# A conditioned expert FFN on one core: two more sets of weights through seven block products

## What is computed

```python
# stage 1, "conditioning": FFN 256 -> 1024 -> 256 with relu, weights corrected by LoRA
# (common and expert factors of rank 16 each; the expert is given per sequence)
Wi = wi + 2 * (common_wi_b @ common_wi_a + experts_wi_b[id] @ experts_wi_a[id])
Wo = wo + 2 * (common_wo_b @ common_wo_a + experts_wo_b[id] @ experts_wo_a[id])
y = relu(x @ Wi.T) @ Wo.T
# stage 2: router on the mean over the tokens, softmax, the two best of 8 experts, shares w
p = softmax(mean(y, tokens) @ gate_w);  (e1, w1), (e2, w2) = top2(p), shares normed to 1
out = x + sum_k w_k * (gelu(y @ w1[e_k] + b1[e_k]) @ w2[e_k] + b2[e_k])
```

## Time and profile before

| what | value |
|---|---|
| median of 3 runs | 270.0 us (268.86 to 270.25) |
| the profiled execution, its time / its span | 269.23 us / 267.4 us |
| busy: PE, PEld | 98%, 80% |
| busy: DVE, ACT, POOL | 61%, 64%, 55% |
| TensorE clock granted, mean | 0.999 |
| DMA, mean rate over the span | 73 to 74 GB/s, 17.43 MB read and 2.10 MB written |

### The profile page before, as it was taken

The page is one execution under the profiler, slowest core; times in us unless marked ns, Lnnn a source line. Parts: engine busy times, 40 slices in busy tenths (PEclk is TensorE's granted clock), DMA queues, the critical chain, the costliest instruction groups (busy, mean ns, idle before and its releaser), DMA issues.

```text
span 267.4 us, 3575 instructions
## 1 busy us (share of the span) xinstructions
PE 262.0 (98%) x1156; PEld 213.4 (80%) x1156; DVE 162.3 (61%) x269; ACT 171.0 (64%) x275; POOL 146.2 (55%) x178
## 2 busy tenths in 40 slices
PE   6999999999999999999999999999999999999994
PEld 2778888888888888888888788888788888888883
DVE  0883624323498826667595787557866567665664
ACT  2757334455526469988986887676677676774650
POOL 2176244373836877798539999466356366331100
PEclk9999999999999999999999999999999999999999
DMA  5995120210032012202202112203202105000004
GB/s 175 357 388 194 42 78 0 82 39 2 0 122 78 6 73 79 81 1 78 81 0 58 37 67 78 78 0 79 70 12 80 66 15 196 0 0 4 0 0 157
DMA packets 11138, 19.75 MB, mean 74 GB/s; under 512 B 2000, under 2 KB 2256, under 8 KB 10992
## 3 DMA queue, kind: packets, MB, share of 16 engines
q1 hardware_dynamic: 10544, 18.61, 21.0%
q10 hardware_dynamic: 576, 0.92, 1.0%
HBM read 17.43 MB, written 2.10 MB: 73 GB/s over the span
## 4 chain that ended last, share of the span: by engine, by line
PE 96%; DMA 1%; SPq 1%; DVE 0%; issue 0%; DVEq 0%
PE out_ps L693 16%; PE out_ps L694 16%; PE out_ps L697 16%; PE hid_ps L693 14%; PE hid_ps L694 14%; PE hid_ps L697 14%; DMA lora_first<-in_early 1%; PE hid_ps L736 1%; PE out_ps L814 1%; PE hid_ps L740 1%; PE hid_ps L744 1%; PE hid_ps L826 1%; PE hid_ps L836 1%; SPq L296 1%; DVE x_sb L1133 0%
## 5 line engine op out<-in xcount | busy, mean ns | idle before, releaser
L398 POOL TENSOR_TENSOR up_lo<-up_raw,up_hi 128x512 fp32r<-128x512 f32 x39 | 50.6, 1316 | 51.4 <-ACT up_hi L529 51.4
L693 PE MATMUL out_ps<-hid_hi,down_hi 128*128 128x512 f32 x192 | 74.9, 390 | 0.0
L694 PE MATMUL out_ps<-hid_lo,down_hi 128*128 128x512 f32 x192 | 74.8, 389 | 0.0
L697 PE MATMUL out_ps<-hid_hi,down_lo 128*128 128x512 f32 x192 | 74.8, 389 | 0.0
L693 PE MATMUL hid_ps<-act_hi,up_hi 128*128 128x512 f32 x168 | 65.8, 391 | 0.0
L694 PE MATMUL hid_ps<-act_lo,up_hi 128*128 128x512 f32 x168 | 65.6, 390 | 0.0
L697 PE MATMUL hid_ps<-act_hi,up_lo 128*128 128x512 f32 x168 | 65.4, 389 | 0.0
L561 ACT ACTIVATE hid_ps<-hid_ps,bias_sb 128x512 f32<-128x512 f32 x64 | 42.2, 659 | 29.6 <-DVE hid_ps L981 19.1
L957 DVE SCALAR_TENSOR_TENSOR hid_lo<-hid_ps,mix,hid_hi 128x512 fp32r<-128x512 f32 x64 | 47.8, 747 | 18.7 <-ACT hid_hi L575 18.2
L404 POOL TENSOR_TENSOR down_lo<-down_raw,down_hi 128x512 fp32r<-128x512 f32 x24 | 31.6, 1317 | 41.4 <-ACT down_hi L539 41.3
L575 ACT ACTIVATE hid_hi<-hid_ps,mix 128x512 fp32r<-128x512 f32 x64 | 44.1, 689 | 4.6
(11 more groups left out here) (89 smaller groups left out, 214.0 us busy)
## 6 DMA issues: line engine op xcount, KB each, us to landing
up_raw<-in_w SPq DMA_DIRECT2D x16, 256.0 KB, 2.8
down_raw<-in_w SPq DMA_DIRECT2D x16, 256.0 KB, 2.6
lora_raw<-in_lora SPq DMA_DIRECT2D x10, 256.0 KB, 5.3
down_raw<-in_woT SPq DMA_DIRECT2D x8, 256.0 KB, 3.5
up_raw<-in_wiT SPq DMA_DIRECT2D x7, 256.0 KB, 4.6
outT<-x_sb SPq DMA_DIRECT2D x6, 256.0 KB, 3.6
x_sb<-in_xT SPq DMA_DIRECT2D x1, 1024.0 KB, 8.9
x_sb<-in_xT SPq DMA_DIRECT2D x1, 512.0 KB, 5.8
```

What stands on the lines that cost most here:

```text
L398: ins = eng.tensor_tensor(up_lo[:, n, cols], up_raw[:, n, cols], f32(up_hi[:, n, cols]), ALU.subtract)
L693: eng.matmul(out, w_h, a_h, start=start, stop=False, skip_group_check=onto)
L694: eng.matmul(out, w_h, a_l, start=False, stop=False, skip_group_check=onto)
L697: return eng.matmul(out, w_l, a_h, start=False, stop=stop, skip_group_check=onto)
```

## The change

Sets 4 and 5 become seven sets too. For that:

- the token sums of sequence 1 are made on POOL in sets 1 and 2, their high parts on ACT in set 2, their low parts on DVE in set 3; all four `raw_low` of sequence 1 stand in set 2;
- `weight_sums(4)` and `weight_sums(5)` stand on POOL in sets 2 and 3, behind the merge of their LoRA product, and the up product of set 4 is made in set 2 (a second up factor there) and that of set 5 in set 3;
- in a seven set of the conditioning the factor products and the logits stand at other places in PE's order (down factor after down pair 2), and use bank 0 instead of 3;
- the router's reduction out of bank 0 gets a semaphore of its own (`s_read`), and the rest of that step (`router_max`) comes later;
- ACT's and DVE's order in sets 4 and 5 is written anew, and POOL's in sets 1 to 4.

```diff
-    PLAIN = range(N_COND)
+    PLAIN = [n for n in range(N_COND) if n not in (SETS, SETS + 1)]
     PLAIN_TILES = [(0, 0), (1, 0), (0, 1), (1, 1)]
...
+    UP_FACTOR_AT = {0: [1], 1: [2], 2: [3, 4], 3: [5], 5: [6], 6: [7]}
     PRODUCTS = []
     for n in range(N_COND):
-        if n + 1 < N_COND:
-            PRODUCTS.append(("u", n + 1))
-        PRODUCTS.append(("d", n))
+        ups = [("u", to) for to in UP_FACTOR_AT.get(n, ())]
+        PRODUCTS += ups[:1] + [("d", n)] + ups[1:]
...
+    def products_to(q):
+        return max(product_count("d", q), *(product_count("u", to) for to in UP_FACTOR_AT.get(q, [1])))
...
     RAW_HI_AT = {1: [(0, 0), (0, 1)], 5: [(1, 0), (1, 1)], 9: [(2, 0)], 10: [(2, 1)]}
-    RAW_LO_AT = {2: [(0, 0), (0, 1)], 3: [(0, 2), (0, 3)], 6: [(1, 0), (1, 1), (1, 2), (1, 3)],
+    RAW_LO_AT = {2: [(0, 0), (0, 1), (0, 2), (0, 3)], 6: [(1, 0), (1, 1), (1, 2), (1, 3)],
                  11: [(2, 0), (2, 1)], 12: [(2, 2), (2, 3)]}
-    SUM_AT = {5: [(1, 0), (1, 1), (1, 2), (1, 3)], 9: [(2, 0), (2, 1)], 10: [(2, 2), (2, 3)]}
-    SUM_HI_AT = {6: [(1, 0), (1, 1)], 12: [(2, 0)], 13: [(2, 1)]}
-    SUM_LO_AT = {7: [(1, 0), (1, 1), (1, 2), (1, 3)], 13: [(2, 0), (2, 1)], 14: [(2, 2), (2, 3)]}
-    LORA_HI_AT = {1: [(0, 4)], 2: [(1, 0), (1, 1)], 3: [(1, 2), (1, 3)], 4: [(1, 4)]}
-    LORA_LO_AT = {0: [(0, 2)], 1: [(0, 4)], 2: [(1, 0)], 3: [(1, 1), (1, 2)], 4: [(1, 3), (1, 4)]}
+    SUM_AT = {1: [(0, 0), (0, 1)], 2: [(0, 2), (0, 3)], 5: [(1, 0), (1, 1), (1, 2), (1, 3)], 9: [(2, 0), (2, 1)], 10: [(2, 2), (2, 3)]}
+    SUM_HI_AT = {2: [(0, 0), (0, 1)], 6: [(1, 0), (1, 1)], 12: [(2, 0)], 13: [(2, 1)]}
+    SUM_LO_AT = {3: [(0, 0), (0, 1), (0, 2), (0, 3)], 7: [(1, 0), (1, 1), (1, 2), (1, 3)], 13: [(2, 0), (2, 1)], 14: [(2, 2), (2, 3)]}
+    LORA_HI_AT = {1: [(0, 4), (1, 0)], 2: [(1, 2), (1, 1)], 3: [(1, 3)], 4: [(1, 4)]}
...
+        s_read = sem("s_read")
...
             b = READY_SEQ[p]
-            eng.wait_ge(s_sum_hi, 2 * (p - 1) + m // 2 + 1)
+            eng.wait_ge(s_sum_hi, 2 * p + m // 2 + 1)
             eng.tensor_tensor(act_lo[:, b, 4 + m, :], t_sum[:, m, :], f32(act_hi[:, b, 4 + m, :]),
...
                 w, n = up_raw[:, q % NU, :], q % NU
-                eng.wait_ge(s_up_raw[n], 16 * (q // NU + 1))
+                if cond(q):
+                    eng.wait_ge(s_merge, product_count("u", q))
+                else:
+                    eng.wait_ge(s_up_raw[n], 16 * (q // NU + 1))
                 eng.tensor_tensor(w[:, block(S3)], w[:, block(0)], w[:, block(1)], ALU.subtract)
...
                 if m == 0:
-                    eng.wait_ge(s_y, NT * KD * p)
-                    if p > 1:
-                        eng.wait_ge(s_sum_lo, 4 * (p - 1))
+                    if p == 0:
+                        eng.wait_ge(s_x1, 16)
+                    else:
+                        eng.wait_ge(s_y, NT * KD * p)
+                        eng.wait_ge(s_sum_lo, 4 * p)
                 if m in (2, 3):
-                    eng.wait_ge(s_t, 4 * (p - 1) + (1 if m == 2 else 3))
+                    eng.wait_ge(s_t, 4 * p + (1 if m == 2 else 3))
                 left = [(0, 1), (1, 1), (1, 1), (1, 0)][m]
...
-            def lora_lows(q):
-                for b, lot in LORA_LO_AT.get(q, ()):
-                    lora_low(b, lot)
...
             after((s_down_lo, 1))
-            lora_lows(0)
+            lora_low(0, 2)
             for q in range(1, NSET):
-                if q < N_COND - 1:
+                if q == 1:
+                    up_low(2)
+                    down_low(1)
+                    after((s_down_lo, 2))
+                    lora_low(0, 4)
+                    token_sums(1)
+                    after((s_t, 2))
+                    lora_low(1, 0)
+                elif q == 2:
+                    up_low(3)
+                    token_sums(2)
+                    down_low(2)
+                    after((s_down_lo, 3))
+                    lora_low(1, 2)
+                    weight_sums(4)
+                elif q == 3:
+                    up_low(4)
+                    weight_sums(5)
+                    down_low(3)
+                    after((s_down_lo, 4))
+                    lora_low(1, 1)
+                    lora_low(1, 3)
+                elif q == 4:
+                    up_low(5)
+                    down_low(4)
+                    after((s_down_lo, 5))
+                    lora_low(1, 4)
+                elif q < N_COND - 1:
                     if q in TOTAL_AT:
...
                     token_sums(q)
-                    if q in LORA_LO_AT:
-                        after((s_down_lo, q + 1))
-                        lora_lows(q)
                 elif q == N_COND - 1:
...
                 if b and t == 0:
-                    eng.wait_ge(s_t, 4)
+                    eng.wait_ge(s_t, 8)
                     eng.wait_ge(s_raw_lo, 8)
...
                 b = READY_SEQ[p]
-                eng.wait_ge(s_t, 4 * (p - 1) + 2 * (n + 1))
+                eng.wait_ge(s_t, 4 * p + 2 * (n + 1))
                 eng.activation(act_hi[:, b, 4 + 2 * n:6 + 2 * n, :], t_sum[:, 2 * n:2 * n + 2, :], ACT.Copy)\
...
                         up_high(q + 1)
+                    if q == SETS:
+                        up_high(q + 1)
                 if q - 2 in GROUP_LAST[0:NB]:
...
                         term_high(LOGITS_AT[q])
-                    up_high(q + 1)
-                    hid_high(q, 1)
-                    down_high(q)
                     if q - 1 in GROUP_LAST[0:NB]:
                         cond_out(GROUP_LAST.index(q - 1), 0)
-                    hid_high(q, 2)
+                    if seven(q):
+                        hid_high(q, 1)
+                        if q > SETS:
+                            up_high(q + 1)
+                        hid_high(q, 2)
+                        down_high(q)
+                    else:
+                        up_high(q + 1)
+                        hid_high(q, 1)
+                        down_high(q)
+                        hid_high(q, 2)
                     if q + 1 == N_COND:
...
                 if bank == 0 and q - 1 in LOGITS_AT:
-                    eng.wait_ge(s_nmax, LOGITS_AT[q - 1] + 1)
-                if bank == 3 and 1 <= q < N_COND:
-                    eng.wait_ge(s_merge, product_count("d", q))
+                    eng.wait_ge(s_read, LOGITS_AT[q - 1] + 1)
+                if bank == 0 and 0 < q <= N_COND and seven(q - 1):
+                    eng.wait_ge(s_merge, products_to(q - 1))
+                if bank == 3 and 1 <= q < N_COND and not seven(q):
+                    eng.wait_ge(s_merge, products_to(q))
...
                 eng.wait_ge(s_up_hi, q)
-                if q == SETS:
-                    eng.wait_ge(s_raw_lo, 4)
-                if q == N_COND:
-                    eng.wait_ge(s_raw_lo, 8)
-                    eng.wait_ge(s_sum_lo, 4)
-                if q == N_COND + TOP_K * SETS:
-                    eng.wait_ge(s_raw_lo, 12)
-                    eng.wait_ge(s_sum_lo, 8)
+                if q in GROUP_FIRST[1:]:
+                    eng.wait_ge(s_raw_lo, 4 * GROUP_FIRST.index(q))
+                    eng.wait_ge(s_sum_lo, 4 * GROUP_FIRST.index(q))
...
+            def factors_to(q):
+                bank = 0 if seven(q) else 3
+                return hid_ps[:, bank, :], (s_hid_lo, 4 * q + 1 if seven(q) else 4 * q)
             def next_up_factor(q):
-                if q + 1 < N_COND:
-                    eng.wait_ge(s_hid_lo, 4 * q)
-                    up_factor(q + 1, hid_ps[:, 3, 0:SW], hid_ps[:, 3, SW:2 * SW])
+                bank, free = factors_to(q)
+                for to in UP_FACTOR_AT.get(q, ())[:1]:
+                    eng.wait_ge(*free)
+                    if q in LOGITS_AT and seven(q):
+                        eng.wait_ge(s_read, LOGITS_AT[q] + 1)
+                    up_factor(to, bank[:, 0:SW], bank[:, SW:2 * SW])
...
                 if q < N_COND:
-                    if q + 1 < N_COND:
-                        eng.wait_ge(s_merge, product_count("u", q + 1))
+                    bank, free = factors_to(q)
+                    if q in UP_FACTOR_AT:
+                        eng.wait_ge(s_merge, product_count("u", UP_FACTOR_AT[q][0]))
                     else:
-                        eng.wait_ge(s_hid_lo, 4 * q)
-                    down_factor(q, hid_ps[:, 3, :])
+                        eng.wait_ge(*free)
+                    down_factor(q, bank)
+            def later_up_factor(q):
+                bank, _ = factors_to(q)
+                for to in UP_FACTOR_AT.get(q, ())[1:]:
+                    eng.wait_ge(s_merge, product_count("d", q))
+                    up_factor(to, bank[:, 0:SW], bank[:, SW:2 * SW])
...
                     down(q - 1, 1)
+                    if cond(q):
+                        router_logits(q)
                     one_of_seven(q, "m5", 3, True)
+                    if cond(q):
+                        next_up_factor(q)
```

(42 more changed lines are left out.)

## The result

The changed kernel took 272.43 us in the median (270.37 to 275.02, 16 runs), the kernel before in the same session 270.25 (268.86 to 273.33, 16 runs). The ratio is 1.0061, with a 95% interval of 1.0031 to 1.0090: slower, by 0.8 to 2.4 us. Three runs of the changed kernel and one of the kernel before lie over 1.5% above the fastest of their kernel and don't count in the ratio; without them the medians are 272.10 and 270.25. Forecast were 272.1 us and "slower by over 0.5%" as the likeliest case.

What follows compares the result with a forecast made beforehand. PE, busy 98% of the span, was taken as the bound. New waits less the removed matmuls gave +1.64 us, POOL in set 4 +0.5: +2.1 on the median 270.0, so 272.1 us, range 269.6 to 273.4.

Steps and rivals of the forecast that it cites:

- Removed: Sets 4 and 5 on PE: two up products fewer, 6 matmuls, 1.36 us saved.
- Logits: Set 5: PE waits 0.25 us ahead of the router logits for hid_low(5,0), which stands behind third_sum(5) on DVE.
- Up factor 7, by raw_high on ACT: Set 6: hid_high(5,3), queued behind two raw_high, comes later; PE waits 0.77 us.
- The chain beside the token sums: Set 6: the router's tiny DVE operations wait for POOL's token sums, putting merge_up(7) at 78.12.
- The open price: Router's two-input DVE operation in set 6: net +0.2 if it passes POOL, +1.64 us if it waits; the wait was taken.
- Down factor 6: Set 6: PE waits 1.90 us for merge_up(7), which follows the router's stretched chain on DVE.
- Last up tile: Set 6: PE waits 0.36 us for merge_down(6), which follows merge_up(7) by 3.33 us on DVE.
- POOL in sets 1 to 4: POOL's added work and collisions with eight DVE lows make PE wait 0.5 us at down pair 0 of set 4.
- Rival 1: Few collisions: router's chain not stretched, POOL in time in set 4; 269.8 to 270.7 us, chance 0.27.
- Rival 2: Set 6: hid_high(5,3) on ACT isn't late and PE never waits; 268.6 us, chance 0.08.
- Rival 3: POOL bounds already in sets 3 and 4, collisions at their upper end; 272.9 to 273.8 us, chance 0.15.
- set 6 lasted its old 11.4 us: Sign on PE's timeline: set 6 keeping its earlier length of 11.4 us would show the prediction wrong.

Runs made afterwards that it cites:

- set4_only: Changed kernel with set 5 plain again, so only set 4 takes seven products; ratio to the kernel before 0.9984, stretch on PE 0.68 us shorter.
- pool_raw_swap: Changed kernel with token sums sooner on POOL, raw_high later on ACT, and hid_low(5,0) ahead of third_sum(5) on DVE; median 268.64 us, ratio to the kernel before 0.9947.
- pool_early: Changed kernel with POOL's token sums of set 5 sooner, three ahead of up_low(6), the fourth ahead of down_low(5); ratio to the kernel before 0.9962.
- before_tok_late: Kernel before with POOL's four token sums of set 5 held until hid_low(5,3) is done; ratio to the kernel before 1.0099.
- raw_late: Changed kernel with ACT's two raw_high of set 5 moved behind hid_high(6,0); ratio to the kernel before 1.0057.
- before_b: Kernel before, unchanged, in a second profiled execution; stretch on PE 60.13 us against 60.15 in the first.

## Why the prediction was right, and where not

The time (272.1 against 272.43) and the sign were right, and so was the way there, but for one term: 0.5 us of wait for POOL in set 4, which did not come. That the time came within 0.3 us is in part luck: without that term the sum gives 271.6, and the ratio puts the changed kernel at 271.9.

- **Removed:** 6 matmuls, 1.36 us. Right: `set4_only` shows half of it, `pool_raw_swap` all.
- **Logits:** a wait of 0.25; measured 0.30.
- **Up factor 7, by raw_high on ACT:** 0.77; measured 0.70 with its aftermath. hid_high(5,3) was forecast 2.11 us behind the start of set 6 and came 1.97 behind (71.48 to 73.45).
- **The chain beside the token sums:** forecast 4.86 us from hid_low(5,3) to merge_up(7), measured 4.77. The open price, whether the two-input operation (L1081) waits for POOL, was settled: 1.00 us, ended with a token sum; 0.23 in `pool_early`. By the Trainium skill's page SBUF — State Buffer (Who interferes with whom) it had to wait, and the trace agrees.
- **Down factor 6:** 1.90; measured 1.79. **Last up tile:** 0.36; measured 0.39. The four waits sum to 3.28 forecast, 3.18 measured.
- **POOL in sets 1 to 4, the term that was mis-sized:** I took 0.5 us of wait at down pair 0 of set 4, "nearer to the upper end". Measured: nothing. down_low(3) ended at 49.87, where PE needed it near 51.5; 1.6 us were in hand. The eight lows on DVE cost POOL far less than the 0.65 each that I took: from lora_low at 25.31 to the end of down_low(3) are 24.56 us, 2.9 more than my count of POOL's work (21.7), so by estimate 0.36 for each of the eight. The timelines show that the two engines shared the price: the low that DVE began at 28.71 took 1.30 us, to 30.01, past the end of POOL's second token sum (29.46), and POOL's lora_low, begun at 29.54, took 1.87 instead of 1.53. In all the eight lows took DVE about 1.9 us more than their own time. `set4_only` confirms that nothing is lost there.
- So the sets came to +1.83 where the forecast had 1.64 + 0.5 (the waits less the matmuls and less 0.1 of an old wait give 1.72; 0.1 I can't place). The ratio's 1.65 us (0.8 to 2.4) holds both.

Rival 1 (few collisions) asked for a chain that isn't stretched; here it was stretched, from 3.60 to 4.77 us. Rival 2 needed ACT 0.8 us sooner. Rival 3 needed a late POOL; it was on time. The prediction was to be wrong if set 6 lasted its old 11.4 us; it lasted 14.35.

What stays open: the rest of the timed difference of `pool_early` (-0.4 us at a full clock, where its stretch says 0.0; the scatter of these runs allows as much), and whether the wait of 1.7 us in the changed kernel ever brings the clock down. In its two profiles it did not, and 11 of its 16 timed runs had a mean clock of 0.998 or more, which leaves no room for a fall of 3.4 us; the other five can have theirs from the start-up.

## What to carry to other kernels

When an edit moves one instruction of the bounding engine later (here a factor product, by 3 us), follow what each other engine has queued behind that instruction's consumer, for a whole stage on. Two engines that wait for one another's instructions, as DVE and POOL do here, need their timelines laid beside one another: a chain of tiny operations that takes 3.0 us alone (`pool_early`) took up to 6.3 beside the other engine's long ones. And cure a wait together with what lies behind it: moving `raw_high` alone brought 0.65 us, both cures with the swap brought 3.3 (all in the stretch).

## What the runs showed of the hardware

- DVE operations with two SBUF inputs (L1081, 227 ns alone) and eight-column TENSOR_SCALARs waited for POOL's current instruction of 1.25 us, and took up to 1.29 us each (`before_tok_late`). What did not wait, in the changed kernel beside POOL's sums: one-column TENSOR_SCALARs (L1084, 0.15 us), reductions (L1080, L1083, 0.16) and `hid_low`, which reads one operand from PSUM (L1015, 0.69). Nor did a two-input operation that came within 0.05 us after the end of a POOL instruction (L1097 in `raw_late`, 0.17 us).
- POOL waits for DVE as well: beside a DVE low with two SBUF inputs its lora_low took 1.87 us instead of 1.53 (changed kernel, at 29.54).
- PE's clock fell to 1.2 GHz after PE had stood 2.1 us without a matmul in `before_tok_late`, and cost 1.7 us more; after a wait of 1.7 us in the changed kernel, in both profiles, and of 1.75 us in `raw_late`, it stayed at 2.4 GHz.
- The start-up of one kernel differs by 4 us between executions (18.46 and 22.55 us to the same instruction), in good part through the granted clock in the first 20 us: 0.50 from 10 to 15 us in `before_b`, 1.00 in the first profile.
